# Large SBUF buffers of a four-stage transformer kernel placed at chosen distances from the split input, modulo 1024 bytes

## Time and profile before

| | |
|---|---|
| median of 3 runs | 2264.07 us (2252.8 to 2265.4) |
| profiled execution | 2264.36 us |
| its span, first to last instruction | 2262.2 us |
| mean granted TensorE clock | 0.971 of 2.4 GHz |
| instructions | 30499 |

### The profile page before, as it was taken

The page is one execution under the profiler, slowest core; times in us unless marked ns, Lnnn a source line. Parts: engine busy times, 40 slices in busy tenths (PEclk is TensorE's granted clock), DMA queues, the critical chain, the costliest instruction groups (busy, mean ns, idle before and its releaser), DMA issues. The chain is left out here.

```text
span 2262.2 us, 30499 instructions
## 1 busy us (share of the span) xinstructions
PE 2151.8 (95%) x11008; PEld 1608.6 (71%) x11008; DVE 1456.9 (64%) x2505; ACT 1208.2 (53%) x2425; POOL 556.9 (25%) x543
## 2 busy tenths in 40 slices
PE   7999999999999999989999969999999799999998
PEld 5888888888888888867787843333333477787886
DVE  4666666666766666656656548888881556645554
ACT  4655556565656565544444334787776334444333
POOL 3433434343334343322222200000000012222221
PEclk9999999999999999999999986999997899999999
DMA  2000000000000000011111110010100011111111
GB/s 80 15 16 16 15 24 15 24 15 24 15 17 15 24 15 15 6 40 42 43 43 42 46 39 13 18 22 16 22 15 1 27 35 42 45 47 43 49 45 59
DMA packets 54297, 64.74 MB, mean 29 GB/s; under 512 B 9179, under 2 KB 34566, under 8 KB 54150
## 3 DMA queue, kind: packets, MB, share of 16 engines
q1 hardware_dynamic: 54150, 62.81, 9.9%
HBM read 52.68 MB, written 2.10 MB: 24 GB/s over the span
## 5 line engine op out<-in xcount | busy, mean ns | idle before, releaser
L812 POOL TENSOR_TENSOR a_pr<-a_pr,a_rinv 128x128 f32<-128x128 f32 (+7 forms) x256 | 294.1, 1149 | 516.6 <-DVE a_rinv L1045 516.5
L1655 DVE TENSOR_REDUCE a_negm<-psum 128x1 f32<-128x1024 f32 x256 | 301.5, 1220 | 49.2 <-PE psum L1533 48.4
L1208 POOL TENSOR_TENSOR f_lo_gu<-f_raw_gu,f_hi_gu 128x512 fp32r<-128x512 f32 x84 | 108.8, 1296 | 868.4 <-ACT f_hi_gu L1294 868.4
L1636 ACT ACTIVATE a_pt<-psum 128x512 f32<-128x512 f32 x512 | 268.3, 602 | 91.1 <-PE psum L1548 90.8
L69 PE MATMUL psum<-xh,f_hi_gu 128*128 128x512 f32 x672 | 272.1, 405 | 6.5 <-DVE f_hid L1366 5.9
L1377 DVE TENSOR_TENSOR f_hl<-f_hid,f_hh 128x512 fp32r<-128x512 f32 x168 | 116.7, 694 | 241.5 <-ACT f_hh L1319 239.7
L71 PE MATMUL psum<-xh,f_lo_gu 128*128 128x512 f32 x672 | 266.4, 396 | 0.0
L70 PE MATMUL psum<-xl,f_hi_gu 128*128 128x512 f32 x672 | 266.2, 396 | 0.0
L1308 ACT ACTIVATE f_act_s<-psum,f_bias 128x512 f32<-128x512 f32 x168 | 115.1, 685 | 282.7 <-PE psum L71 282.6
L961 ACT ACTIVATE a_pth<-psum 128x512 fp32r<-128x512 f32 (+3 forms) x384 | 174.8, 490 | 143.9 <-PE psum L868 141.2
L954 ACT ACTIVATE a_pr<-psum,a_negm 128x128 f32<-128x128 f32 (+7 forms) x256 | 190.3, 743 | 80.2 <-DVE a_negm L1036 75.8
(11 more groups left out here) (299 smaller groups left out, 4754.0 us busy)
## 6 DMA issues: line engine op xcount, KB each, us to landing
f_raw_gu<-in_gu SPq DMA_DIRECT2D x84, 256.0 KB, 2.8
f_raw_dn<-in_down SPq DMA_DIRECT2D x84, 128.0 KB, 2.0
a_wr<-in_qkv SPq DMA_DIRECT2D x32, 256.0 KB, 2.8
a_wvr<-in_qkv SPq DMA_DIRECT2D x32, 128.0 KB, 2.6
a_wor<-in_o SPq DMA_DIRECT2D x32, 128.0 KB, 2.0
a_qq<-x_qhi SPq DMA_DIRECT2D x128, 32.0 KB, 1.9
yT<-in_xT SPq DMA_DIRECT2D x4, 512.0 KB, 6.5
a_qq<-x_qlo SPq DMA_DIRECT2D x64, 32.0 KB, 1.9
```

Of the source, the lines that this page charges most:

```text
L812: pool.tensor_tensor(pr[j][:, 0:n], pr[j][:, 0:n], rinv[:, j:j + 1].to_broadcast([P, n]), ALU.mult).then_inc(p_done, 1)
L1636: act.activation(pt[:, s % SLOTS, g, :], st_ps[:, n % 3, :], ACT.Exp, scale=1.0 / HD1).then_inc(exp_done, 1)
L1655: dve.tensor_reduce(negm[:, u % 2, g * NQ + q:g * NQ + q + 1], mx_ps[:, bank, :, :], AX.XY, ALU.max, negate=True).then_inc(mx_taken, 1)
```

## The change

The change moves buffers in SBUF. `Phase` now counts the bytes of a partition that have been handed out since `xh` (`Phase.top`), and `level(offset)` allocates a filler, which nothing uses, so that the next buffer begins at `offset` modulo 1024 bytes from the start of `xh`. Causal attention calls it with 0 ahead of its buffers, both mixtures with 768, grouped attention with 0, and the phase `x`, which holds `ks`, `vs`, `qhi`, `qlo`, with 0 behind `wqkv`. Buffers whose rows are no multiple of 1024 bytes, or small, go to the end of their group: `bias` and the `b2` buffers in the mixture behind `cmap`, `cTh` and `cTl`; in grouped attention `pt` comes directly behind `qq`. No instruction, wait or DMA is added or removed.

```diff
--- before.py
+++ after.py
@@ -31,11 +31,20 @@
 NSH0, NSH1 = -(-HS0 // P), -(-HS1 // P)
 
 
+def row_bytes(shape):
+
+    return -(-4 * int(np.prod(shape[1:])) // 32) * 32
+
+
 class Phase:
 
 
 
+    LINE = 1024
+    top = 0
+
     def __init__(self, nc, tag, psum=None):
+        self.floor = Phase.top
         self.nc, self.tag, self.stack, self.psum, self.bank = nc, tag, ExitStack(), psum, 0
 
     def __enter__(self):
@@ -43,8 +52,16 @@
 
     def __exit__(self, *a):
         self.stack.close()
+        Phase.top = self.floor
+
+    def level(self, offset):
+
+        gap = (offset - Phase.top) % Phase.LINE
+        if gap:
+            self.sb(f"level{Phase.top}", [P, gap // 4])
 
     def sb(self, name, shape, dt=F32):
+        Phase.top += row_bytes(shape)
         return self.stack.enter_context(self.nc.sbuf_tensor(f"{self.tag}_{name}", shape, dt))
 
     def ps(self, shape):
@@ -651,6 +668,7 @@
         return [(0, CQ, n), (CQ, qt + 1 - CQ, n + 1)]
 
     with Phase(nc, tag, psum) as ph:
+        ph.level(0)
         wr = ph.sb("wr", [P, 2, 2, DT, E0])
         wh = ph.sb("wh", [P, 2, 2, DT, E0], F32R)
         wl = ph.sb("wl", [P, 2, 2, DT, E0], F32R)
@@ -1112,8 +1130,8 @@
     NC = S // CH
 
     with Phase(nc, tag, psum) as ph:
+        ph.level(768)
         raw_gu = ph.sb("raw_gu", [P, 2, 2 * DT * P])
-        bias = ph.sb("bias", [P, NT, 2])
         hi_gu = ph.sb("hi_gu", [P, 2, 2 * DT * P], F32R)
         lo_gu = ph.sb("lo_gu", [P, 2, 2 * DT * P], F32R)
         raw_dn = ph.sb("raw_dn", [P, 2, D])
@@ -1124,6 +1142,11 @@
         hid2 = ph.sb("hid2", [P, NC, CH])
         hh = ph.sb("hh", [P, 2, NC, CH], F32R)
         hl = ph.sb("hl", [P, 2, NC, CH], F32R)
+        cmap = ph.sb("cmap", [P, routers[0].rw.nmap, T])
+        held = B if biased else 1
+        cTh = [ph.sb(f"cTh{b}", [ne + 1, S], F32R) for b in range(held)]
+        cTl = [ph.sb(f"cTl{b}", [ne + 1, S], F32R) for b in range(held)]
+        bias = ph.sb("bias", [P, NT, 2])
         if biased:
             b2 = ph.sb("b2", [ne + 1, D])
             b2h = ph.sb("b2h", [ne + 1, D], F32R)
@@ -1131,10 +1154,6 @@
             b2_in = ph.sem("b2_in")
             b2_hi = ph.sem("b2_hi")
             b2_lo = ph.sem("b2_lo")
-        cmap = ph.sb("cmap", [P, routers[0].rw.nmap, T])
-        held = B if biased else 1
-        cTh = [ph.sb(f"cTh{b}", [ne + 1, S], F32R) for b in range(held)]
-        cTl = [ph.sb(f"cTl{b}", [ne + 1, S], F32R) for b in range(held)]
         for b, r in enumerate(routers):
             r.into(cmap, cTh[b % held], cTl[b % held])
         gate_ps = ph.ps([P, CH])
@@ -1419,12 +1438,13 @@
     W = VW
 
     with Phase(nc, tag, psum) as am:
+        SLOTS = 4
+        am.level(0)
         qq = am.sb("qq", [P, QSLOT, 2, CH], F32R)
-        SLOTS = 4
+        pt = am.sb("pt", [P, SLOTS, G1, CH])
         LAG = 2
         negm = am.sb("negm", [P, 2, G1 * NQ])
         mrow = am.sb("mrow", [G1 * NQ, 2, P], F32R)
-        pt = am.sb("pt", [P, SLOTS, G1, CH])
         zt = am.sb("zt", [P, CH])
         rden = am.sb("rden", [P, NQ, G1])
         mx_ps = am.ps([P, 2, 2, CH])
@@ -1795,6 +1816,7 @@
             rw1 = RouterWeights(g, "rw1", w1, False)
             with Phase(nc, "x") as x:
                 wqkv = Projection(x, "wqkv", a["wqkv1"], a["bqkv1"])
+                x.level(0)
                 ks = [x.sb("ks0", [P, 2, S], F32R)]
                 vs = [x.sb("vs0", [P, S // P, G1, VW])]
                 qhi = [x.sb("qhi0", [P, 2, S], F32R)]
```

## The result

| | before | after |
|---|---|---|
| median of 10 executions | 2264.1 us (2252.8 to 2265.5) | 2242.0 us (2238.0 to 2251.6) |
| ratio | | 0.991, interval 0.9893 to 0.9926 |
| profiled execution | 2264.36 us | 2240.75 us |
| its span, mean granted clock | 2262.2 us, 0.971 | 2238.6 us, 0.977 |

I forecast 2255 us. The kernel became 22.1 us faster, more than twice the 9.5 us of my sum.

What follows compares the result with a forecast made beforehand. TensorE, busy 95% of the time, was taken as the bound, so spacing of matmuls counts outside grouped attention. Terms of 3.1 + 5.9 + 0.5 = 9.5 us less from 2264.36 gave 2255 us, range 2240 to 2268.

Steps and rivals of the forecast that it cites:

- rival 3: All matmuls lock to the fast rhythm of 227.5 ns and less: 25 us less, 2239 us; chance 0.13.
- Term (b): Gate and up matmuls in both mixtures fall to 392 ns if the pattern repeats every 256 bytes: 5.9 us less.
- Term (a): Causal attention's q, k and v projections become cheaper at distance 0/512: 3.1 us less.
- (c): Transposes of pr in causal attention, 276 ns, cost the same after pr moves against ident: 0.
- (d): Grouped attention, where pt against vs goes from 128 to 0: 0.5 us less.
- (e): VectorE, ScalarE and GpSimd don't feel the moved buffers, and GpSimd's subtraction is hidden: 0.
- rival 1: Distance has no effect; the kind of task makes the 2 to 4 ns: 2264 us; chance 0.15.
- 2 (period of 512): 256/768 is like its neighbours, so only causal attention gains 3.1 us, and 0.5: 2261 us; chance 0.18.
- 4 (256/768 the worst): Gate and up in the mixtures cost 7.2 us more at 398.5 ns, less 3.1: 2268 us; chance 0.10.
- 5 (the counted top goes wrong): Counted top and real address part, so every loop gets a chance distance: 2.8 us less, 2262 us; chance 0.04.

Runs made afterwards that it cites:

- e12: The changed kernel itself, unaltered, measured again beside e11 on the same chip: 2252.5 us, ratio 0.9946.
- e4: Changed kernel with both mixtures' buffers at 0 instead of 768: 2252.6 us, ratio 0.9937.
- e5: Changed kernel with the first mixture at 832 and the second at 960 instead of 768 (64 and 192 modulo 256): 2251.8 us, one execution.
- e6: Changed kernel with the first mixture at 640 and the second at 544 instead of 768 (128 and 32 modulo 256): 2264.7 us, one execution.
- e10: Changed kernel with a 96-byte filler between hid2 and hh, moving hidden activations against their weights: mixtures 322.2 and 461.6 us.
- e1: Kernel before with only the mixtures' part of the change (768, bias last), both attentions as before: 2242.7 us, ratio 0.9907.
- e3: Kernel before with only phase x and grouped attention moved to 0, causal attention and mixtures as before: 2263.3 us, ratio 0.9981.
- e8: Kernel before plus two unused 512-column matmuls in each of grouped attention's last 24 slots: 2257.9 us, ratio 0.9976.
- e7: Changed kernel plus two unused 512-column matmuls in each of grouped attention's last 24 slots: 2247.6 us, ratio 0.992.
- e11: Changed kernel plus one unused 512-column matmul in each of grouped attention's last 24 slots: 2244.7 us, ratio 0.9911.
- e2: Kernel before with only causal attention's buffers moved to 0, everything from the first mixture on as before: 2253.3 us, ratio 0.9955.
- e9: Changed kernel with a 96-byte filler ahead of xh, moving every buffer equally: 2243.4 us, one execution; mixtures 318.2 and 454.4 us.

## Why the prediction was wrong, and where it was right

**What the change does itself.** Compare executions of equal mean clock, over all occasions: at 0.977 the kernel before took 2252.4 us and the changed one 2239.6 to 2241.3; at 0.971 2262.6 to 2265.4 against 2249.8 to 2250.6; at 0.967 2270.2 to 2272.8 against 2256.9 to 2257.1. That is 11 to 16 us each time, and the stages say the same: 4.5 + 6.9 in the mixtures and 1.6 in causal attention, 13.0. Beside e12, where both kernels mostly lost the clock, the medians differ by 12.5 us (2265.0 and 2252.5). The other 9 us of the first 22.1 are that 8 of 10 executions of the changed kernel kept the clock and, by its time, 1 of 10 before. That 2242.0 lies near my rival 3 (2239) is luck: its 25 us were to come from matmuls alone, and 9 of the 22 did not.

**Term (b), gate and up: right in kind, too small.** The pattern does repeat every 256 bytes (e4, e5, e6), which I had taken from three points of a curve, and 0 is its lowest point. The size was 11.4 us and not 5.9, of which gate and up alone, by the fall of their durations to 390, make 816 x 5.5 + 1200 x 4.5 = 9.9. I priced 0/512 with 392 ns, the mean over groups from 390 to 393 that lay there before, a spread as large as the effect; and I called it cheaper in three stages where the earlier trace rows show two. Those groups stood in loops whose other matmuls were at bad distances, and e10 shows that a neighbour at a bad distance slows the others. With every kind at 0 the loop has 389 to 390, and the down projections, which I had left at their old price since they "move together", gain as well: 393 to 389 in the first mixture. This is what rival 3 said, in the mixtures; its 25 us were too much, since causal attention did not lock.

**Term (a), causal attention: right in sign, too large.** Between the same two matmuls with `xl` and `wh` (line 70 before, 87 after), one of the fifth pair and one of the last, lie 831.5 us before (and 831.6 to 831.7 in e1, e3 and e8, with causal attention at its old place) and 830.0 to 830.2 in the ten kernels with it at 0: 1.3 to 1.6 us less, and not 3.1. By distances between starts in this stretch, the q, k and v projections gain 2.1 to 2.3 us (L70 with `a_wh` 395 to 392 in duration, as forecast). The scores with 512 columns gain 1.0 us more, though `qh`, `ql`, `kh` and `kl` have not moved against each other: the neighbours again. Two things take it back. The shorter matmuls, of 128 to 384 columns, of scores and probabilities times values cost 0.8 to 0.9 us more. And 1.1 us go into waiting, a step that I had left out: between each score tile and its first transpose TensorE adds the mask (line 858), and the idle time behind these matmuls grows from 4.7 or 4.8 us to 5.7 or 5.8. Over the whole stage the idle time ahead of the transposes is 9.5 us in the earlier trace rows and 10.7 in the row above, most of it waiting for `pr` from GpSimd, whose busy time in the stage is the same (377.1 and 377.6 us). That TensorE now only comes earlier to the same wait fits this; no run tests it. The mask's own matmuls hardly change: the 202 of 221 without a wait behind them take 74.4 to 74.5 ns to the next start before and 74.9 after, although `mask` has moved against `idr` as well.

**Terms (c), (d), (e): right.** Transposes of `pr` 276 ns before and after; grouped attention's unit 21.96 and 21.94 us, which is 0.3 us in all, and e3 shows no effect of its addresses on it; the other engines' durations are the same.

**The step that failed most: the clock was not in the sum.** The earlier trace rows shows grouped attention at 0.92, and I passed over it. I took the profiled execution's lengths as those of the kernel, while 10 to 11 us of it were a fall of the clock in the last unit that comes in most executions and not in all. The three times given (2252.8 beside 2264.1 and 2265.4) already showed the two cases; I used them to widen the range only. In this place TensorE has lost the maxima's matmuls, and waits for the exponential. Waits of the kernel before from 1700 us to the end of the stage, and of the kernel after in the same place (us in total, times, longest):
```profile
PEld psum L1548 <- ACT a_pt L1636: 20.1, 24, 1.7
...
PEld psum L1568 <- ACT a_pt L1656: 17.2, 24, 0.9
```
The waits are much the same where the clock fell and where it held, so they alone don't decide whether it falls. e7, e8 and e11 show that more load on TensorE in this place prevents it: 24 of 24 executions with the filling matmuls kept the clock, 9 of 68 of the kernel before did.

**What stays open.** Whether the layout changes the odds of the fall. Without fillers the changed kernel kept the clock in 8 of 10 executions and later in 2 of 12, e1 in 5 of 6, e2 in 7 of 10, e3 in 4 of 10, e4 in 1 of 7. The changed kernel differs from one occasion to the next as much as any two kernels do, so no address can be named for it. Yet something in the layouts may matter: the kernel before kept the clock in 1 of 10, 2 of 24, 3 of 17 and 3 of 17, and beside its 2 of 24, on the same chip, e1 to e4 together kept it in 17 of 33. e2, with nothing moved but causal attention's buffers, is among them. No run settles this, so the changed kernel's 0.991 holds 9 us that its 0.9946 does not, and which I can only call luck.

**The rivals.** 1 (no effect of distance) and the order of the buffers are refuted by e5, e6, e9 and e10. What I drew from the Trainium skill there, that addresses don't matter, falls with rival 1. The Trainium skill, TensorE: Matmul & The Clock Gate, section Step-by-step: what each phase is for, says that loading the next weights takes no read bandwidth from the running matmul, because the two read ports are independent. The measurements differ from it, by 227 to 228 ns against 233 for the same matmuls of the first mixture at a granted clock of 1.00, in e4 and e5, which differ there in nothing but the distance between the two, and they decide. Why the distance matters inside the chip no run shows. 2 (period of 512) and 4 (256/768 the worst) fall with e4. 5 (the counted top goes wrong) falls with the forecast of e6's second mixture, off by 0.4 us. 3 holds for the mixtures.

## What to carry to other kernels

Where TensorE is the bound and its matmuls follow each other closely, look at the distance between the start of what streams and the weights that are loaded meanwhile: here 0 modulo 256 bytes gave 227 to 228 ns for 512 columns and other distances 230 to 235, and one buffer at a bad distance slows its neighbours in the loop. Place odd-sized buffers last. And read the granted clock at the end of a stage, over several executions: where TensorE's work thins out, 10 us can hang on it, and a change measured over few executions can be credited or charged with them.

## What the runs showed of the hardware that was not expected

- The spacing of 512-column matmuls at a granted clock of 1.00 depends on operand distance modulo 256 bytes, also while all other engines are idle: 390 ns of duration at 0, 395 to 396 at 32 and 64, 394 to 395 at 128, 397 to 399 at 160 (down projections only), 391 to 392 at 192.
- The cost spreads: in e10 gate and up rose by 2 to 4 ns though only their neighbours' operand had moved.
- 128-column products show next to nothing of it: the transposes of `pr` stay at 276 ns and the mask's products at 74.4 to 74.9 ns to the next start, though both moved against their other operand.
- A gain ahead of a wait is partly lost in it: of some 3 us that 512-column matmuls gave in causal attention, 1.1 us went into idle time ahead of the transposes.
- 24 matmuls of 512 columns and no use cost 1 to 2 us and kept, in 6 of 6 executions, a clock whose fall costs 9 to 11.
